# Regrouping the attention stage of a two-layer graph network: where a chunk's scatters, clears, products and table loads stand

## The reference, cut to what matters

```python
q = qkv[:, 0] * SCALE
scores = jnp.einsum('ehd,ehd->eh', q[src], k[dst])
m = jax.ops.segment_max(scores, dst, num_segments=n)
e = jnp.exp(scores - m[dst])
s = jax.ops.segment_sum(e, dst, num_segments=n)
sa = e / s[dst]
he = (v[src] * sa[:, :, None]).reshape(-1, D)
agg = jax.ops.segment_sum(he, dst, num_segments=n)
```

## Time and profile before

| what | value |
|---|---|
| median of the three runs | 3718.84 us |
| profiled execution, its span | 3706.35 us, 3704.5 us |
| mean granted TensorE clock over the span | 0.851 of full speed |
| attention, 305 to 1718 us | 1413 us, PE busy 1218.65 us, DVE 977.01 us, ACT 471.72 us, POOL 803.49 us, clock 0.88, DMA share 0.65 |

### The profile page before, as it was taken

One profiled execution on the slowest core, in us unless ns is written; L12 is line 12 of the kernel. 1 busy time (PEld: TensorE's weight loads), 2 busy tenths in 40 slices (PEclk: granted clock), 3 DMA queues, 4 the chain that ended last, 5 costly groups with the idle time before them and its releaser, 6 DMA issues. The chain is left out here.

```text
span 3704.5 us, 52330 instructions
## 1 busy us (share of the span) xinstructions
PE 3044.7 (82%) x13207; PEld 1951.2 (53%) x13207; DVE 2203.3 (59%) x4818; ACT 972.8 (26%) x2518; POOL 1596.5 (43%) x1665
## 2 busy tenths in 40 slices
PE   3786888888888888884899799999967777777775
PEld 2444555555555555552799688888733333333332
DVE  5775676767766766774887422222265556555555
ACT  0442333333333333332666333333300000000000
POOL 0115656555655555550000000000077777777775
PEclk7887899989989989896999899999976777677776
DMA  2336766666666666662322444444453333333334
GB/s 73 113 118 203 208 192 192 186 184 190 195 178 186 188 180 187 183 179 68 102 101 80 140 183 191 188 184 192 180 183 105 105 105 105 105 105 105 106 105 141
DMA packets 233805, 557.05 MB, mean 150 GB/s; under 512 B 48397, under 2 KB 128353, under 8 KB 220994
## 3 DMA queue, kind: packets, MB, share of 16 engines
q0 software_dynamic: 104144, 324.24, 31.3%
q1 hardware_dynamic: 111706, 197.31, 14.7%
q10 hardware_dynamic: 17688, 32.15, 2.7%
HBM read 402.88 MB, written 150.70 MB: 149 GB/s over the span
## 5 line engine op out<-in xcount | busy, mean ns | idle before, releaser
L1147 POOL DMA_INDIRECT rel_rows<-msg_d,msg_i_again x783 | 744.5, 951 | 852.6 <-DMA msg_i_again<-msg_i_d 614.2
L767 POOL DMA_INDIRECT qv_rows<-qv_d,src_i x832 | 803.5, 966 | 580.3 <-PE out_ps L1039 390.4
L1167 PE MATMUL rel_ps<-rel_rows,rel_hot 128*128 x1664 | 751.4, 568 | 244.8 <-SPq L1135 178.5
L1039 PE MATMUL out_ps<-qv_rows,hot 128*128 128x264 f32 x1664 | 658.4, 481 | 83.2 <-DVE qv_rows L845 75.4
L1167 PEld LDWEIGHTS rel_ps<-rel_rows,rel_hot 128*128 128x128 f32 x1664 | 359.1, 257 | 636.7 <-issue 623.4
L1192 DVE TENSOR_TENSOR sums_all<-sums_all,rel_ps 128x256 f32 x832 | 350.6, 421 | 401.2 <-PE rel_ps L1167 351.7
L1688 PE MATMUL ms_mm<-wrel,ms_hTs 128*128 128x512 f32 x2352 | 560.6, 397 | 3.3 <-DVE wrel L1635 2.9
L1688 PEld LDWEIGHTS ms_mm<-wrel,ms_hTs 128*128 128x128 f32 x2352 | 440.7, 189 | 103.5 <-issue 3.8
L791 DVE TENSOR_TENSOR qv_rows<-qv_rows,kx 128x512 f32<-128x512 f32 x416 | 283.0, 680 | 347.5 <-PE kx L989 338.2
L989 PE MATMUL kx<-k,hot_t 128*128 x2496 | 409.2, 303 | 12.1 <-issue 6.8
L931 ACT COPY at_acc<-out_ps 128x264 f32 x832 | 313.9, 378 | 358.3 <-PE out_ps L1039 263.5
(11 more groups left out here) (198 smaller groups left out, 2557.3 us busy)
## 6 DMA issues: line engine op xcount, KB each, us to landing
msg_d<-msg SPq DMA_DIRECT2D x98, 1024.0 KB, 3.9
dl_b<-dlt_d ACTq DMA_DIRECT2D x50, 512.0 KB, 3.7
qv_rows<-qv_d,src_i POOLq DMA_INDIRECT x832, 3.7
qv_d<-qv SPq DMA_DIRECT2D x7, 1820.0 KB, 6.5
rel_rows<-msg_d,msg_i_again POOLq DMA_INDIRECT x783, 2.8
agg_d<-at_acc SPq DMA_DIRECT2D x49, 132.0 KB
up_agg<-agg_d SPq DMA_DIRECT2D x7, 924.0 KB, 4.9
xg<-in_x_dram SPq DMA_DIRECT2D x7, 896.0 KB, 9.4
```

The lines of the kernel that those rows point to most:

```text
L767: nc.gpsimd.indirect_dma_start(rows[:, n % SLOTS, :], None, qv_d, bass.IndirectOffsetOnAxis(ap=src_i[:, n:n + 1], axis=0)).then_inc(got[n ...
L1039: nc.tensor.matmul(out_ps[:, bass.ds(bank, AGGW)], hot[:, s, :], rows[:, slot(k, s), FEAT:], start=False, stop=True, skip_group_check=True ...
L1147: nc.gpsimd.indirect_dma_start(rows[:, at:at + FEAT], None, table, bass.IndirectOffsetOnAxis(ap=msg_i[:, e:e + 1], axis=0)).then_inc(got[e ...
L1167: nc.tensor.matmul(sum_ps[n % BANKS][:], hot[:, n % HOTS, :], rows[:, bass.ds(at, FEAT)], start=True, stop=True).then_inc(summed, 1)
```

## The change

No arithmetic is changed, and no instruction is added or removed but for waits and register work. What moves:

- PE: the scatters 10 to 15 of chunk k - 2 (six, instead of 13 to 15) stand in the chain of chunk k - 1; `turn_hot(k - 1, 0)` and `turn_hot(k - 1, 2)` and the expansions 4 and 5 stand before the first scatter of chunk k - 1. The scatter and its clear become two functions, and something may stand between them. The expansions 0 and 1 of chunk k + 1 stand between the last four scatters of the loop.
- DVE: the first product of chunk k + 1 stands at the end of loop k; `head_sums(k, 0)` stands between `step_maxima` and `carries`; `values` 1, 2 and 3 stand together; `places(k + 1)` stands behind them and ahead of products 6 and 7.
- ACT: the four loads stand apart (first steps after `columns`, breaks after the second `turned_back`, flags after the evacuation of step 15, places after the evacuation of step 1 of the following chunk). First steps and flags are loaded one loop later than before, one loop ahead of their use. Table values are read one step earlier, before the last evacuation of a quad or two.

```diff
@@ vector, loop k @@
+                product(0, 0)
                 for k in range(ROUNDS + 1):
-                    if now:
-                        product(k, 0)
                     if before:
                         step_maxima(k - 1)
                     if now:
                         product(k, 1)
+                        head_sums(k, 0)
                     if before:
                         carries(k - 1)
...
                         values(k - 1, 0)
                     if now:
-                        head_sums(k, 0)
-                    if before:
-                        values(k - 1, 1)
-                    if now:
                         product(k, 4)
                         product(k, 5)
                         head_sums(k, 1)
                     if before:
-                        values(k - 1, 2)
+                        for quad in range(1, QUADS):
+                            values(k - 1, quad)
+                    if k + 1 < ROUNDS:
+                        places(k + 1)
                     if now:
                         product(k, 6)
-                    if k + 1 < ROUNDS:
-                        places(k + 1)
-                    if before:
-                        values(k - 1, 3)
-                    if now:
                         product(k, 7)
                         head_sums(k, 2)
                         head_sums(k, 3)
+                    if k + 1 < ROUNDS:
+                        product(k + 1, 0)
@@ scalar, loop k @@
                     if before:
+                        evacuate(k - 2, banks, UNROLL - 4)
                         evacuate(k - 2, banks, UNROLL - 3)
                     if now:
                         columns(k - 1)
+                    if 2 <= k < ROUNDS:
+                        load_first_steps(act, k)
+                    if now:
+                        turned_back(k - 1, 0)
                     if before:
                         evacuate(k - 2, banks, UNROLL - 2)
                     if now:
                         exponents(k - 1)
-                        if k + 1 < ROUNDS:
-                            load_segments(act, k + 1)
-                            act.wait_ge(hot_ok, k)
-                            load_places(act, k + 1)
+                        turned_back(k - 1, 1)
+                    if further:
+                        load_breaks(act, k + 1)
                     if before:
                         evacuate(k - 2, banks, UNROLL - 1)
-                        if now:
-                            banks = banks_of(k - 1, 0)
+                    if 2 <= k < ROUNDS:
+                        load_flags(act, k)
                     if now:
-                        for quad in range(QUADS - 1):
-                            turned_back(k - 1, quad + 1)
-                            evacuate_quad(k - 1, banks, quad)
-                            banks = banks_of(k - 1, quad + 1)
-                        if k < ROUNDS:
-                            turned_back(k, 0)
-                        evacuate(k - 1, banks, UNROLL - QUAD)
+                        banks = banks_of(k - 1, 0)
+                        evacuate(k - 1, banks, 0)
+                        evacuate(k - 1, banks, 1)
+                    if further:
+                        act.wait_ge(hot_ok, k)
+                        load_places(act, k + 1)
+                    if now:
+                        evacuate(k - 1, banks, 2)
+                        following = banks_of(k - 1, 1)
+                        evacuate(k - 1, banks, 3)
+                        banks = following
+                        turned_back(k - 1, 2)
+                        evacuate(k - 1, banks, 4)
+                        evacuate(k - 1, banks, 5)
+                        turned_back(k - 1, 3)
+                        following = banks_of(k - 1, 2)
+                        evacuate(k - 1, banks, 6)
+                        evacuate(k - 1, banks, 7)
+                        banks = following
+                        evacuate(k - 1, banks, 8)
+                        following = banks_of(k - 1, 3)
+                        for s in range(9, 12):
+                            evacuate(k - 1, banks, s)
+                        banks = following
@@ tensor, loop k, as it is after the change (late = a scatter of chunk k-2, early = one of chunk k-1) @@
                     if before:
                         turn_scores(k - 1)
                     if old:
+                        clear(late(10))
+                        step = late(11)
                     if before:
                         turn_ends(k - 1)
+                    if old:
+                        clear(step)
+                    if before:
+                        turn_hot(k - 1, 0)
+                    if old:
+                        step = late(12)
                     if now:
                         expand(k, tiles, 2)
                     if old:
+                        clear(step)
+                        clear(late(13))
                     if before:
                         carry_columns(k - 1)
                     if now:
                         expand(k, tiles, 3)
+                    if old:
+                        clear(late(14))
                     if before:
                         turn_hot(k - 1, 1)
+                    if old:
+                        clear(late(15))
+                    if before:
                         turn_probs(k - 1)
                     if now:
                         expand(k, tiles, 4)
                     if before:
+                        turn_hot(k - 1, 2)
                     if now:
                         expand(k, tiles, 5)
                     if before:
+                        for s in range(3):
+                            clear(early(s))
+                        step = early(3)
                     if now:
                         expand(k, tiles, 6)
                     if before:
+                        clear(step)
+                        clear(early(4))
+                        step = early(5)
                         turn_hot(k - 1, 3)
+                        clear(step)
                     if now:
                         expand(k, tiles, 7)
+                    if before:
+                        clear(early(6))
+                        step = early(7)
...
+                    if following:
+                        expand(k + 1, ahead, 0)
+                    if before:
+                        clear(step)
+                        clear(early(8))
+                        step = early(9)
+                    if following:
+                        expand(k + 1, ahead, 1)
+                    if before:
+                        clear(step)
```

More of the change, by code:

```diff
@@ L737, in load_places, with load_breaks @@
                 eng.dma_start(dl_b[:, k % 2], dl_rows[:, t0 * P:(t0 + UNROLL) * P].to_broadcast([P, UNROLL * P])).then_inc(dl_ld[k % 2], 16)
[L739 removed]
+            def load_breaks(eng, k):
                 t0 = k * UNROLL
@@ L742, in load_segments, with load_flags, load_first_steps @@
                               ).then_inc(seg_ld[k % 2], 16)
+            def load_flags(eng, k):
                 eng.dma_start(flag[:, k % 2], fl_d[k:k + 1, :]).then_inc(seg_ld[k % 2], 16)
-                eng.dma_start(hb[:, k % 2], hb_d[t0:t0 + 1, :]).then_inc(seg_ld[k % 2], 16)
+            def load_first_steps(eng, k):
+                eng.dma_start(hb[:, k % 2], hb_d[k * UNROLL:k * UNROLL + 1, :]).then_inc(seg_ld[k % 2], 16)
             @block.sync
@@ L750, in _ @@
                     load_places(sp, k)
-                    load_segments(sp, k)
+                    load_breaks(sp, k)
+                    load_flags(sp, k)
+                    load_first_steps(sp, k)
                 for t in range(NODE_TILES):
@@ L931, in evacuate @@
                     nc.scalar.copy(acc[:, at:at + AGGW], out_ps[:, bass.ds(banks[s % QUAD], AGGW)]).then_inc(acc_ok, 1)
-                def evacuate_quad(k, banks, quad):
-                    for q in range(QUAD):
-                        evacuate(k, banks, QUAD * quad + q)
                 act.wait_ge(init_ok, 1)
-                turned_back(0, 0)
-                banks = banks_of(0, 0)
                 for k in range(1, ROUNDS + 2):
                     now, before = k <= ROUNDS, k >= 2
+                    further = k + 1 < ROUNDS
                     if now:
@@ L1023, in turn_probs @@
                     nc.tensor.transpose(p_ps[:], probs[:], ident[:]).then_inc(p_ok, 1)
-                def scatters(k, tiles, first, end, ahead, chunk_ahead):
-                    for s in range(first, end):
-                        scatter(k, tiles, s, ahead, chunk_ahead)
                 def scatter(k, tiles, s, ahead, chunk_ahead):
@@ L1041, in scatter, with clear @@
                     load_tiles(ahead, chunk_ahead, 1)
+                    return n, odd
+                def clear(step):
+                    n, odd = step
```

(28 more changed lines are left out.)

5 lines of the change are left out of this document (removed).

## The result

The changed kernel takes 3457.84 us, median of 4 runs (3451.81 to 3463.14), against 3717.68 for the kernel before, also 4 runs: ratio 0.929, interval 0.927 to 0.932, 260 us less. The profiled execution takes 3463.14 us with a span of 3461.3, 243 us under the one before. Forecast was 3522, so the sign and the mechanism held and the size was 64 us short.

The account below looks back on a forecast made before the run. PE leads, with idle time and a lower clock as losses. 26.66 - 23.05 = 3.6 us a chunk, times 51, is 184 us off 3706.35: 3522 us. Range 3425 to 3640; the forecast's own range 3451 to 3575.

Parts of the forecast that it names:

- The three terms of a chunk: Chunk of 26.66 us before: 21.0 PE work at full clock, 3.45 PE idle, 2.2 lost to the lower clock.
- The clock: PE's clock falls only after the chain with its idle gaps; chain filled, 2.2 us a chunk saved, clock near 1.00.
- what is left is 21.0 us of PE work at full clock: PE's work a chunk, 26.66 less 3.45 idle and 2.2 for the clock.
- Load of the places: DVE's `places` newly waits for its load, issued at 12.0 us and taken to land in 6.4 us.
- the crowded row: Landing of 6.7 us seen in the first chunks, where POOL gathers back to back; the 6.4 was taken near it.
- The term of 1.75 us: PE's loss a chunk before expansion 0 of the next chunk, waiting for `places` and product 6; landing less 4.65.
- The chain: From turning of the scores to scatter 0: grows from 9.3 to 10.05 us, with PE working throughout.
- 0.5 us of slack: If DVE were 0.5 us late at the weighting before scatter 0, PE would still not wait.
- POOL: POOL's waits for scatters that free slots fall from 8.2 us a chunk to about 3.
- The landing in time: Rival: the places load lands in under 4.65 us; 21.3 us a chunk, 3433 us in all; chance 0.20.
- slower: Rival: the landing of the places grows further; at 11.5 us a chunk takes 28.15 us, 3782 in all; chance 0.06.
- no change: Rival: DVE passes small waits on to PE, clock low, period near 26.5 us; 3700 us; chance 0.07.

Follow-up runs that it names:

- three in the chain: Changed kernel with three scatters instead of six in the next chunk's chain (10, 11 and 12 back in their own loop): 3612.1 us, 0.971 to the kernel before.
- the control: Changed kernel, unedited, run beside its edits in group 2: 3918.5 us, ratio 0.943 to the kernel before.
- Late and early loads: Changed kernel with the places load behind the evacuation of step 4 (0.963), or right behind the first steps' load (0.948, 0.946); ratios to the kernel before.
- the run that took it away: Changed kernel with the early places load and, on DVE, the first weighting ahead of the rescaling: 3947.8 us, 0.948 to the kernel before.
- the run with the loads together: Changed kernel with ACT's flags, first steps and places loads issued directly behind the breaks load: 3911.4 us, 0.941 to the kernel before.

## Why the prediction was right, and where it was off

*Period, idle time, lower clock.* The three terms of a chunk were 26.66 = 21.0 + 3.45 + 2.2. After: 21.80 = 20.4 + 1.42 + 0. So of 4.86 us the idle time gave 2.0, the clock 2.2, and 0.6 came from work that got shorter. The 2.2 is the prediction's estimate, and the 0.6 hangs on it. The two traces give it in another way: from start to start of PE's pieces of work, idle time taken off, a chunk holds 23.1 us before and 20.3 after; with each piece at the value that a fifth of its instances stay under, 20.5 and 20.0. By that estimate the clock gave some 2.3 us and shorter work 0.5. The kernel with three in the chain fits the same account: 24.68 - 3.62 idle leaves 21.06, a clock of 0.97 is 6% of the time at the lower level, 1.5 us, of which 0.42 is lost: 0.6, and 20.4 again.

*The clock.* I gave 2.2 us as saved with one argument, that the falls come behind the chain. It held: 1.00, and the granted clock falls once in 46 chunks, where it fell 48 times in 49. "At no other place of the chunk", read from one chunk in the earlier trace rows, was too strong: 29 of those falls come 9 to 12 us behind the turning of the scores, near the wait for the weighting, and 19 earlier, within the chain. All are in the stretch that the change filled. That the clock does not follow the sum of idle time, the three-scatter kernel and the control show; no run changed the clock alone, so its price is an estimate.

*Work of PE.* Step that failed: "what is left is 21.0 us of PE work at full clock", carried over unchanged. I had costed the moved clears at nothing. A scatter followed by an expansion needs 0.55 us, one followed by its clear 0.64, and in the old order each expansion stood behind the clear. Six scatters a chunk (11, 12, 3, 5, 7 and 9) now have something between them and their clear, four of them an expansion; at 0.1 us or so each they would make most of the 0.6. That is a sum from rows; no run moved the clears alone.

*Load of the places.* The mechanism was right, its size wrong: "I take 6.4 us for the landing" measured 4.96 in the median. I had put it near the crowded row, a row of the first chunks; around those loads (340 to 347 and 366 to 373 us) the DMA share was 0.86 and 0.82, above the 0.78 seen after. With 4.96 at 11.5 us `places` starts at 16.5, and my own formula, landing less 4.65, gives 0.3; PE waits 0.39. The term of 1.75 us in my sum was the main miss, 1.36 us a chunk too much, partly set off by 0.7 us of small waits that I had left out of the sum: those for the carries and the weighting (0.55), and gaps too short for the list of waits. (The upper end of the forecast's own range, 23.35 and 0.7 us, is 3573 and not 3575.) Late and early loads show that the path is real and that removing the rest of the wait gives nothing measurable under the pauses.

*The chain.* Laid out at 10.05 us, measured 9.98. The 0.5 us of slack that I gave PE at the weighting was not there: it waits 0.32 us in every chunk. PE is through with expansion 5 at 9.7 us (laid out: 10.05), and the weighting ends at 9.75 (laid out: 9.6), behind a rescaling that waits 0.59 for the clear of step 15. Whether that wait costs anything is not shown; the run that took it away, under the pauses, was not faster.

*POOL.* Waits of about 3 us forecast, 3.2 measured.

*Parts.* More than half of the gain hangs on the three further scatters in the chain. I had argued DVE's regrouping and ACT's spreading as parts that fit; the runs show that neither is needed, ACT's under the pauses only. That leaves PE's order, together with ACT's order of copies, evacuations and table reads, which has to follow it; no run had PE's order alone, or DVE's and ACT's changes undone at once.

*Rivals.* The landing in time (3433) lay nearer than my forecast; slower and no change are out.

## What to carry to other kernels

When a dependent chain alternates between engines, count what PE can do in it that does not depend on it, and put the remainder of the previous round there; changing the order of the other engines alone can cost more than it brings. Test each engine's reordering by itself: here the gain stood without DVE's reordering, and DVE's reordering alone cost 9%. Take a transfer's landing from rows with the load that the changed kernel will have, not from the extreme row.

## What was not expected of the hardware

A load issued among back-to-back gathers, at a DMA share of 0.78, landed 4.96 us after its issue in the median (4.60 to 6.51, 47 chunks), against 3.7 in the median before and 6.4 to 6.7 in two of its first chunks. The issue of the breaks' load took 0.61 us where it took 1.10 before, with the same 32 KB. In the run with the loads together, where it is again the first of four issued back to back, it took 1.10 in all 39 chunks of 400 to 1400 us; in the runs with the loads apart it comes behind that of the first steps and took 0.61. So it goes with where it stands, though no run says why. And the same kernel took 3720 us in one group and 4156 in another, on the same chip, with pauses of about 2 us on PE; what makes them stays open.
